# Building the transposed activations on the tensor engine, and seven smaller edits, in a four-layer hybrid block on eight cores

## The reference

```python
x = x + attn_a(layernorm(x))      # random-feature attention, biases
x = x + ffn(layernorm(x))
x = x + attn_b(layernorm(x))      # attention over the feature axis of each head
x = x + ffn(layernorm(x))

def attn_a(x):                    # 16 heads, d_k 64, m 256 random features
    phi = lambda t: (exp(t @ orf.T / d_k**0.25 - |t|^2 / (2 sqrt(d_k))) + 1e-6) / sqrt(m)
    num = phi(q) @ (phi(k).T @ v);  den = phi(q) @ sum_l phi(k)
    return (num / den) @ Wo.T + bo
def attn_b(x):                    # per head: a 64 x 64 matrix
    z = softmax(q.T @ k / 8) @ v.T;  return merge(z) @ Wo.T
def ffn(x):
    x = x + mla(rmsnorm(x))       # 16 heads, latent 256, rope, causal softmax, @ W_o
    x = x + moe(rmsnorm(x))       # a shared expert and 7 routed ones, top 2, each 1024 wide
    return x
```

## Time and profile before

| | us |
|---|---|
| three runs | 7655.79, 7818.19, 8169.56 |
| median | 7818.19 |
| the profiled execution | 7674.71 |
| its span, slowest core | 7673.1 |
| its span, fastest core | 7603.3 |
| PE busy | 5135.9 (67% of the span) |
| DVE busy | 2376.6 (31%) |
| ACT busy | 1443.4 (19%) |
| POOL busy | 110.9 (1%) |
| share of PE in the chain that ended last | 59% |

### The profile page before, as it was taken

One profiled execution on the slowest core, in us unless ns is written; L12 is line 12 of the kernel. 1 busy time (PEld: TensorE's weight loads), 2 busy tenths in 40 slices (PEclk: granted clock), 3 DMA queues, 4 the chain that ended last, 5 costly groups with the idle time before them and its releaser, 6 DMA issues.

```text
span 7673.1 us, 81520 instructions; the slowest of 8 cores (7603.3 to 7673.1 us)
## 1 busy us (share of the span) xinstructions
PE 5135.9 (67%) x21088; PEld 2001.2 (26%) x21088; DVE 2376.6 (31%) x5188; ACT 1443.4 (19%) x2520; POOL 110.9 (1%) x147
## 2 busy tenths in 40 slices
PE   2556553565662487999994863565662487999996
PEld 0222221111110233444442321111110233444442
DVE  2333334424222313222223354424222313222221
ACT  1222220242441101011111010242441101011110
POOL 0000000000000000000000000000000000000000
PEclk9556566676775798999997976676775798999996
DMA  5001023001003541222224123000003531122113
GB/s 122 4 6 17 15 36 104 9 10 23 8 11 68 110 66 23 34 43 36 34 34 97 24 31 104 9 9 18 15 11 68 110 66 23 34 39 39 34 34 88
DMA packets 390938, 319.38 MB, mean 42 GB/s; under 512 B 277889, under 2 KB 292737, under 8 KB 390530
## 3 DMA queue, kind: packets, MB, share of 16 engines
q0 software_dynamic: 73584, 145.83, 11.7%
q1 hardware_dynamic: 316946, 168.34, 9.0%
HBM read 287.70 MB, written 79.82 MB: 48 GB/s over the span
## 4 chain that ended last, share of the span: by engine, by line
PE 59%; DVE 11%; ACT 8%; issue 8%; DMA 7%; SPq 3%; DVEq 2%; ACTq 1%; POOL 0%; POOLq 0%
PE PS L210 59%; ACT SCF L220 6%; DVE SCF L215 3%; SPq L78 3%; DVE SCB L215 2%; DVE SM L215 2%; ACT SCA L220 2%; DVE XNT L215 2%; DMA d_xn<-SCF 1%; DMA SCB<-d_yraw 1%; DVEq L73 1%; DVE SCA L215 1%; DMA d_lo<-SCB 1%; DVE STAT L215 1%; SPq L79 1%
## 5 line engine op out<-in xcount | busy, mean ns | idle before, releaser
L210 PE MATMUL PS<-XNT,WB 128*128 128x512 bf16 x9472 | 2093.1, 385 | 610.8 <-DVE XNT L215 436.5
L210 PEld LDWEIGHTS PS<-XNT,WB 128*128 128x128 bf16 x9472 | 936.0, 99 | 1761.7 <-issue 694.7
L210 PE MATMUL PS<-WB,SCA 128*128 128x512 bf16 x4864 | 1101.5, 390 | 358.6 <-DMA SCA<-d_y 272.7
L220 ACT ACTIVATE SCF<-PS,SM 128x512 bf16<-128x512 f32 (+3 forms) x1280 | 773.1, 622 | 1083.6 <-PE PS L210 1011.5
L210 PE MATMUL PS<-SCF,SCA 128*128 128x512 bf16 x1280 | 608.0, 475 | 417.5 <-DVE SCF L215 203.2
L215 DVE TENSOR_TENSOR SCA<-SCA,PS 128x512 bf16<-128x512 bf16 x512 | 351.8, 687 | 1441.8 <-PE PS L210 1337.7
L220 ACT ACTIVATE SCA<-PS 128x512 bf16<-128x512 f32 x640 | 374.8, 595 | 2191.6 <-PE PS L210 1952.0
L210 PEld LDWEIGHTS PS<-WB,SCA 128*128 128x128 bf16 x4864 | 482.2, 100 | 968.6 <-issue 453.4
L210 PE MATMUL PS<-XNT,SCA 128*128 128x512 bf16 x1280 | 615.9, 494 | 11.9 <-DVE SM L215 9.5
L215 DVE SCALAR_TENSOR_TENSOR R<-PS,STAT,R 128x512 f32<-128x512 f32 x448 | 315.7, 746 | 519.1 <-PE PS L210 519.1
L215 DVE TENSOR_TENSOR SCF<-SCF,CONSTB 128x128 bf16<-128x128 bf16 x512 | 106.1, 207 | 975.8 <-ACT SCF L220 971.5
(11 more groups left out here) (119 smaller groups left out, 2389.6 us busy)
## 6 DMA issues: line engine op xcount, KB each, us to landing
WB<-wg_r POOLq DMA_DIRECT2D x28, 1024.0 KB, 13.2
WB<-wu_r POOLq DMA_DIRECT2D x28, 1024.0 KB, 23.6
WB<-wd_r POOLq DMA_DIRECT2D x28, 1024.0 KB, 12.8
d_xn<-SCF SPq DMA_DIRECT2D x96, 256.0 KB, 2.1
sp_x<-R SPq DMA_DIRECT2D x8, 2048.0 KB, 17.3
R<-sp_x POOLq DMA_DIRECT2D x8, 2048.0 KB, 27.6
R<-x SPq DMA_DIRECT2D x4, 2048.0 KB
SCA<-XNT SPq DMA_DIRECT2D x32, 256.0 KB, 3.3
```

The costliest lines, as they stand in the source:

```text
L210: return e.matmul(out_ap, lhsT, rhs, start=start, stop=stop, tile_position=tp)
L220: return getattr(e, name)(*a, **kw)
```

## The change

1. **Transposes on PE.** A new `xnt_tile_transpose(i, v_slot)` follows each tile's normalisation: 8 matmuls with the slot as stationary operand and a bf16 identity `IDENTB` as moving one (128 columns each), 4 to a bank, and 2 DVE copies of 128 x 512 from PSUM to `XNT`. It replaces `xnt_read` at all six places; `xnt_gain` does the multiplication by the gain alone. The dump to `d_xn` stays only in the MoE, for the router. The slot is freed by the matmuls (or in the MoE by the dump, which now waits for the tile's matmuls and copies too).
2. **Key features of attn_a** in 8 steps of two matmuls and 512 columns. ACT takes the exponential without bias; DVE multiplies by the exponential of the bias (once per head by ACT into `STAT[:, 16:32]`) and adds the constant, in one operation per 256 columns. The bank is freed by DVE.
3. **Dumps to `d_yraw`** go from SP to POOL, under a semaphore of their own, `s_yd`.
4. **Tail, first part.** The read of tile `l` waits for the last head's dump of query block `l // 4` only; the scale goes to `STAT` and not to `SM0`.
5. **Tail, second part.** 16 reads of 1024 x 128 in two halves of the tokens, each waiting for the one before it (`(s_tp, s_tp.v)`); PE waits for a half at a time.
6. **Softmax of attn_b** in 8 steps on 128 partitions.
7. One more small load at the start (`IDENTB`).

The diff, cut:

```diff
@@ norm_apply_fused
             v_op("tensor_scalar", slot, xc, STAT[:, 32 + i:33 + i],
                  STAT[:, 96 + i:97 + i], ALU.subtract, ALU.mult, wait=w)
+            v_slot = s_dv.v
             p.drain("vector")
             v_op("tensor_scalar", xc, xc, STAT[:, 32 + i:33 + i],
                  STAT[:, 80 + i:81 + i], ALU.subtract, ALU.mult)
-            vd = s_dv.v
-            p.dma("sync", APx(d_xn, i * 128 * D, [[D, 128], [1, D]]), slot,
-                  s_pp[i % 2], wait=[(s_dv, vd)])
-            p.release(f"xds{i % 2}", s_pp[i % 2])
-        return (s_pp[0].v, s_pp[1].v)
+            xnt_tile_transpose(i, v_slot,
+                               w_extra=([(s_sc, vsc)] if i == 0 else ()))
+            p.release(f"xds{i % 2}", s_mm)
+        p.drain("vector")
+        return s_dv.v
@@ norm_apply_dump
+            v_slot = s_dv.v
             if lo_dump:
...
+            vm_tp = xnt_tile_transpose(i, v_slot,
+                                       w_extra=([(s_sc, vsc)] if i == 0 else ()))
             if dump:
                 vd = s_dv.v
                 p.dma("sync", APx(d_xn, i * 128 * D, [[D, 128], [1, D]]), slot,
-                      s_pp[i % 2], wait=[(s_dv, vd)])
+                      s_pp[i % 2], wait=[(s_dv, vd), (s_mm, vm_tp)])
...
+            else:
+                p.release(f"xds{i % 2}", s_mm)
@@ new
+    def xnt_tile_transpose(i, v_slot, w_extra=()):
+        slot = SCF[:, (i % 2) * D:(i % 2) * D + D]
+        bks = (0, 1) if i % 2 == 0 else (2, 3)
+        vals = []
+        for half in range(2):
+            bk = bks[half]
+            w0 = p.use(f"ps{bk}") + [(s_dv, v_slot), (s_ld, v_preload)]
+            for j in range(4):
+                c = 4 * half + j
+                mm(PS[bk][:, 128 * j:128 * j + 128],
+                   slot[:, 128 * c:128 * c + 128], IDENTB[:, :],
+                   start=True, stop=True, wait=(w0 if j == 0 else ()))
+            vals.append(s_mm.v)
+        for half in range(2):
+            bk = bks[half]
+            src = APx(PS[bk], 0, [[512, 128], [128, 4], [1, 128]])
+            dst = APx(XNT, S * 4 * half + 128 * i, [[NT * D, 128], [S, 4], [1, 128]])
+            v_op("tensor_copy", dst, src,
+                 wait=[(s_mm, vals[half])] + list(w_extra if half == 0 else ()))
+            p.release(f"ps{bk}", s_dv)
+        return s_mm.v
@@ phase_attn_a, key features
-                for l in range(NT):
-                    bk = 6 + (l % 2)
...
+                a_op("activation", out=STAT[:, 16:32], in_=STAT[:, 0:16],
+                     func=AF.Exp, wait=[(s_dv, v_nk)])
+                v_eb = s_ac.v
+                for lp in range(8):
+                    bk = 6 + (lp % 2)
...
+                    for j in range(2):
+                        l = 2 * lp + j
+                        mm(bank[:, 256 * j:256 * j + MF],
+                           SCB[hsl, 2048 + 128 * l:2176 + 128 * l],
+                           ORFT[hsl, :], start=True, stop=True,
+                           wait=(w0 if j == 0 else ()))
                     vm = s_mm.v
+                    a_op("activation",
+                         out=SCA[:, eko + 512 * lp:eko + 512 * lp + 512],
+                         in_=bank[:, 0:512], func=AF.Exp,
+                         wait=[(s_mm, vm), (s_ac, v_eb)])
                     va = s_ac.v
+                    for j in range(2):
+                        l = 2 * lp + j
+                        v_op("tensor_scalar",
+                             SCA[:, eko + MF * l:eko + MF * l + MF],
+                             SCA[:, eko + MF * l:eko + MF * l + MF],
+                             STAT[:, 16 + l:17 + l], EPSP, ALU.mult, ALU.add,
+                             wait=[(s_ac, va)])
+                    p.release(f"ps{bk}", s_dv)
@@ phase_mla, end of a query block
-                    p.dma("sync", APx(d_yraw, 64 * gh * S + 512 * qb,
-                                      [[S, 64], [1, 512]]),
-                          SCF[0:64, 1536:2048], s_pp[3], wait=[(s_dv, vd)])
-                    p.dma("sync", APx(d_yraw, (1024 + gh) * S + 512 * qb,
-                                      [[S, 1], [1, 512]]),
-                          SCF[64:65, 1536:2048], s_pp[3])
-                    p.release("stg", s_pp[3])
+                    p.dma("gpsimd", APx(d_yraw, 64 * gh * S + 512 * qb,
+                                        [[S, 64], [1, 512]]),
+                          SCF[0:64, 1536:2048], s_yd, wait=[(s_dv, vd)])
+                    p.dma("gpsimd", APx(d_yraw, (1024 + gh) * S + 512 * qb,
+                                        [[S, 1], [1, 512]]),
+                          SCF[64:65, 1536:2048], s_yd)
+                    p.release("stg", s_yd)
+                    if h2 == 1 and hl == 7:
+                        v_yq[qb] = s_yd.v
@@ phase_mla, tail
-            w = [(s_pp[3], v_yraw), (s_mm, s_mm.v)] if l == 0 else []
+            w = [(s_yd, v_yq[l // 4]), (s_mm, vmm_latdone)]
...
-        for c in range(ND):
-            src = APx(d_y2, c * 128, [[D, S], [1, 128]])
...
+        for half in range(2):
+            for c in range(ND):
+                src = APx(d_y2, half * 1024 * D + c * 128, [[D, 1024], [1, 128]])
+                w = [(s_tp, s_tp.v)]
...
+            if half == 0:
+                v_y2t_h1 = s_tp.v
...
-                w0 = p.use(f"ps{bk}") + [(s_tp, v_y2t), (s_wl[0], vl_wo)]
+                w0 = p.use(f"ps{bk}") + [(s_tp, v_y2t_h1 if l < 8 else v_y2t),
+                                         (s_wl[0], vl_wo)]
@@ phase_attn_b, softmax
-        for h_ in range(H):
-            po = 64 * (h_ % 2)
-            zsl = PS[6][po:po + 64, 64 * (h_ // 2):64 * (h_ // 2) + 64]
+        for c in range(8):
+            zsl = PS[6][:, 64 * c:64 * c + 64]
...
-            v_op("tensor_scalar_mul", SCA[psl, 2048 * (h_ // 2):2048 * (h_ // 2) + 2048],
-                 SCA[psl, 2048 * (h_ // 2):2048 * (h_ // 2) + 2048], SM0[psl, 3:4])
+            v_op("tensor_scalar_mul", SCA[:, 2048 * c:2048 * c + 2048],
+                 SCA[:, 2048 * c:2048 * c + 2048], SM0[:, 3:4])
```

More of the change, by code:

```diff
@@ L382, in norm_apply_dump @@
                 w.append((s_st, v_sp))
-            if kind == "ln" and to_r:
-                v_op("tensor_scalar", xc, xc, STAT[:, 32 + i:33 + i],
-                     STAT[:, 80 + i:81 + i], ALU.subtract, ALU.mult, wait=w)
-                if dump:
-                    p.drain("vector")
-                    v_op("tensor_copy", slot, xc)
-            elif kind == "ln":
+            if kind == "ln":
                 v_op("tensor_scalar", slot, xc, STAT[:, 32 + i:33 + i],
@@ L1024, in phase_mla @@
                        s_tp, wait=w, transpose=True)
-            v_op("reciprocal", SM0[:, 0:16], slot[:, 1024:1040], wait=[(s_tp, vt)])
+            v_op("reciprocal", STAT[:, 112:128], slot[:, 1024:1040],
+                 wait=[(s_tp, vt)])
             p.drain("vector")
@@ L1038, in phase_mla @@
             return True
-        tv = []
-        for c in range(ND):
-            src = APx(d_y2, c * 128, [[D, S], [1, 128]])
-            w = [(s_pp[0], v_y2[0]), (s_pp[1], v_y2[1]),
-                 (s_mm, s_mm.v), (s_dv, s_dv.v)] if c == 0 else ()
-            tv.append(p.dma("sync", SCA[:, c * S:(c + 1) * S], src, s_tp, wait=w,
-                            transpose=True))
-        v_y2t = tv[-1]
+        v_y2t_h1 = 0
+        for half in range(2):
+            for c in range(ND):
+                src = APx(d_y2, half * 1024 * D + c * 128, [[D, 1024], [1, 128]])
+                w = [(s_tp, s_tp.v)]
+                if c == 0 and half == 0:
+                    w += [(s_pp[0], v_y2h1[0]), (s_pp[1], v_y2h1[1]),
+                          (s_mm, vmm_latdone), (s_dv, s_dv.v)]
+                elif c == 0:
+                    w += [(s_pp[0], v_y2[0]), (s_pp[1], v_y2[1])]
+                p.dma("sync",
+                      SCA[:, c * S + 1024 * half:c * S + 1024 * half + 1024],
+                      src, s_tp, wait=w, transpose=True)
+            if half == 0:
+                v_y2t_h1 = s_tp.v
+        v_y2t = s_tp.v
         for l in range(NT):
@@ L1257, in phase_ffn @@
         vst3 = norm_stats("rms", use_rt=True)
[L1258 to L1260 removed]
+        ppv3 = norm_apply_dump("rms", vst3, dump=True, lo_dump=True)
+        v_gain2 = xnt_gain(WLN2)
+        phase_moe(v_gain2, v_gain2, ppv3)
         if stop_after is not None and stop_after == ("moe1" if call == 0 else "zz"):
```

83 lines of the change are left out of this document (44 added, 39 removed).

## The result

| | before | after |
|---|---|---|
| profiled execution, us | 7674.7 | 7557.4 |
| span, slowest core | 7673.1 | 7555.2 |
| span, median of 8 cores | 7645.4 | 7546.2 |
| median of all runs shown | 7900.1 (10 runs) | 7783.8 (9 runs) |
| ratio of undisturbed runs, 95% interval | | 0.9877 (0.9849 to 0.9906) |

In some executions of either kernel the cores of one die or of both show a lower granted clock and take some per cent longer; the medians hold such runs, the ratio leaves them out, and from the executions of experiments 4 (granted clock 0.79), 8 (0.78 on cores 4 to 7) and 9 (0.73) only the stretches named there are read.

A forecast was written before the change was run, and what follows sets the result against it. PE waiting 629.5 us for DVE writing `XNT`, mostly at four openings, was taken as the lead. Terms -4 - 23 - 19 - 35 - 18 - 6 + 27 - 10 + 0.4 gave -88: 7674.7 to 7587 us, range 7500 to 7735.

The follow-up runs named there:

- experiments 4: Changed kernel with the eight `d_y2` reads of a half not waiting for one another: first reciprocal to first add 123.0 and 123.1 us, from 135.4 and 136.9.
- 8: Changed kernel with free `d_y2` reads and the tail's next tile read issued ahead of the store: first reciprocal to first add 83.4 and 83.5 us.
- 9: Changed kernel with `d_yraw` dumps on SP for 15 heads, on POOL for the last: first reciprocal at 0.16 us, gap between pairs 22.45 us.

## What to carry to other kernels

Where a change empties a queue, ask for every transfer left on it what it will now fly beside, not only when it is needed. In a loop of read, work and write over one queue the times of all three add up. Here issuing the next read ahead of the write was worth 40 us a call in sixteen tiles, and taking the waits off independent reads 12; moving the dumps to POOL won 5.3 at the same place. Two edits can depend on each other: the earlier first read paid only with the dumps off SP, and that cost the heads as much again, until only the last head's dumps were moved. And a table of waits names only the last thing waited for, so compare all the rows that a change can turn into one another.

## What the runs showed of the hardware

- A 64 KB store issued by POOL lands in 1.9 us (median of 128), and a wait for it ended some 0.8 us later than for one issued by SP, two stores in a row each time.
- A wait on SP for a semaphore long past its value costs about 0.05 us: two of them moved the next issue from 0.43 to 0.53 us behind the store.
- A 128 x 128 bf16 transpose by matmul costs 0.11 to 0.13 us in a row of 8 or 16, on a TensorE that had stood idle for 1.8 to 1.9 us before each row. The profile gives a granted clock of 1.00 for the opening of attn_a and 0.50 for those of the first MLA and attn_b; eight took 1.01 us in attn_a, 1.01 to 1.08 in the MLA.
- Eight transposing reads of 1024 x 128 in flight at once took 16.5 us from the last store to TensorE, one after another 27.7.
- Four 2 MB stores with four table loads of 512 KB issued beside them took 2 to 4 us longer than with the loads behind them, and a table load landed after 22.5 us (median of four) in place of 5.5.
